# Gated cross-attention and six local-attention layers on one core: a new order of work in a slot, LayerNorm input half in place, logits in pairs

## What is computed

```python
x = x + tanh(g_xattn) * xattn(layernorm(x), ctx, ctx, fside, ...)   # softmax(QK' + bias) V, 16 heads of 8
h = layernorm(x)
for i in range(6):
    h = attn_layer(shift_tokens(h), Wqkv[i], q_scale[i], k_scale[i], Wo[i]) + h
    h = ffn_layer(shift_tokens(h), ln_g[i], ln_b[i], W1[i], b1[i], W2[i], b2[i]) + h
x = x + tanh(g_ffn) * h
# attn_layer: q, k = l2norm(.) * scale, rotary; per window of 32: softmax(8 q k' + mask) v
# ffn_layer: layernorm, W1 -> (a, gate), a * gelu(gate) @ W2;  shift_tokens moves half of the features by one token
```

## Time and profile before

| | |
|---|---|
| median of 3 runs | 2069.49 us (2068.37 to 2073.53) |
| profiled execution, its own time | 2061.48 us |
| its span | 2059.7 us |
| mean granted TensorE clock | 0.972 of 2.4 GHz |
| busy: PE, PEld | 1797.2 us (87%), 1401.8 us (68%) |
| busy: DVE, ACT, POOL | 1600.0 (78%), 1384.6 (67%), 1332.1 us (65%) |
| chain that ended last | PE 60%, DVE 15%, issue 12%, ACT 6%, POOL 5% |

### The profile page before, as it was taken

One profiled execution on the slowest core, in us unless ns is written; L12 is line 12 of the kernel. 1 busy time (PEld: TensorE's weight loads), 2 busy tenths in 40 slices (PEclk: granted clock), 3 DMA queues, 4 the chain that ended last, 5 costly groups with the idle time before them and its releaser, 6 DMA issues.

```text
span 2059.7 us, 86637 instructions
## 1 busy us (share of the span) xinstructions
PE 1797.2 (87%) x33584; PEld 1401.8 (68%) x33584; DVE 1600.0 (78%) x3772; ACT 1384.6 (67%) x3701; POOL 1332.1 (65%) x1226
## 2 busy tenths in 40 slices
PE   6999878998879898789988899988898988899887
PEld 3445457777667776677776677776677776677766
DVE  5766679898468987488896589885689885689984
ACT  3677657777557776567775577775577775577765
POOL 3444467777467777377775477774677773677773
PEclk9999979999989999999999999999899999899999
DMA  5000021111021111111110211110211110211111
GB/s 121 4 5 5 1 70 33 35 37 32 25 64 41 31 36 28 63 34 33 40 31 23 68 40 31 41 31 23 64 44 31 31 42 22 65 37 37 31 33 46
DMA packets 59120, 77.81 MB, mean 38 GB/s; under 512 B 16608, under 2 KB 31674, under 8 KB 57914
## 3 DMA queue, kind: packets, MB, share of 16 engines
q1 hardware_dynamic: 58938, 75.36, 13.9%
HBM read 22.63 MB, written 1.05 MB: 11 GB/s over the span
## 4 chain that ended last, share of the span: by engine, by line
PE 60%; DVE 15%; issue 12%; ACT 6%; POOL 5%; SPq 0%; DMA 0%; DVEq 0%; ACTq 0%; POOLq 0%
PE proj_ps L455 7%; PE s_ps L476 7%; PE tr_ps L465 7%; PE y_ps L524 7%; PE proj_ps L457 5%; PE proj_ps L456 5%; PE y_ps L516 4%; DVE by_cos L1091 3%; PE pv_ps L506 3%; ACT square L816 3%; DVE by_sin L1091 3%; DVE xs L1352 3%; PE s_ps L571 3%; DVE sumsq L1103 2%; PE s_ps L691 2%
## 5 line engine op out<-in xcount | busy, mean ns | idle before, releaser
L1502 POOL TENSOR_TENSOR qk<-by_cos,by_sin 128x512 f32<-128x512 f32 x388 | 495.3, 1276 | 208.3 <-DVE by_sin L1091 201.9
L1509 POOL TENSOR_TENSOR qk<-qk,inv_norm 128x512 f32<-128x512 f32 x388 | 404.8, 1045 | 68.7 <-ACT inv_norm L822 41.6
L1091 DVE TENSOR_TENSOR by_cos<-proj_ps,tab 128x512 f32<-128x512 f32 x364 | 249.4, 685 | 159.6 <-ACT square L816 158.6
L816 ACT ACTIVATE square<-proj_ps 128x512 f32<-128x512 f32 x364 | 217.4, 597 | 195.1 <-PE proj_ps L457 194.8
L1515 POOL TENSOR_TENSOR s_sb<-s_sb,row_max 128x512 f32<-128x512 f32 x192 | 202.7, 1056 | 136.1 <-DVE row_max L1122 136.1
L455 PE MATMUL proj_ps<-w_hi,x_hi 128*128 128x512 f32 x546 | 273.8, 502 | 4.8 <-DVE by_sin L1091 2.6
L465 PE MATMUL tr_ps<-ident,qk 128*128 128x128 f32 x1544 | 247.2, 284 | 24.2 <-ACT x_hi L810 11.8
L1103 DVE TENSOR_REDUCE sumsq<-square 128x8 f32<-128x512 f32 x388 | 262.2, 676 | 0.0
L1091 DVE TENSOR_TENSOR by_sin<-proj_ps,tab 128x512 f32<-128x512 f32 x364 | 247.8, 681 | 0.0
L465 PEld LDWEIGHTS tr_ps<-ident,qk 128*128 128x128 f32 x1544 | 184.0, 146 | 72.5 <-POOL qk L1509 28.5
L457 PE MATMUL proj_ps<-w_hi,x_lo 128*128 128x512 f32 x546 | 222.1, 407 | 0.0
(11 more groups left out here) (172 smaller groups left out, 4167.1 us busy)
## 6 DMA issues: line engine op xcount, KB each, us to landing
arena<-v SPq DMA_DIRECT2D x388, 130.0 KB, 2.4
w_raw<-in_L_ffn_Wqkv SPq DMA_DIRECT2D x7, 1536.0 KB, 7.3
wo<-in_L_ffn_Wo SPq DMA_DIRECT2D x7, 512.0 KB, 3.8
w_raw<-in_L_ffn_W SPq DMA_DIRECT2D x7, 341.0 KB, 5.5
c_in<-in_ctx SPq DMA_DIRECT2D x16, 64.0 KB, 1.8
xn<-in_fside_BxS SPq DMA_DIRECT2D x1, 1024.0 KB, 6.0
out<-z SPq DMA_DIRECT2D x4, 256.0 KB, 3.0
w<-in_L_ffn_W SPq DMA_DIRECT2D x12, 64.0 KB
```

Source lines behind the costliest of these rows:

```text
L1091: return dve.tensor_tensor(dst[:, c % 2, :].rearrange("p (h d) -> p h d", d=DH), ps, tb, ALU.mult)
L1502: pool.tensor_tensor(heads(qk[:, c, :]), heads(by_cos[:, c % 2, :]), heads(by_sin[:, c % 2, :])[:, :, ::-1, :], ALU.add).then_inc(qk_added, 1)
L1509: pool.tensor_tensor(ap, ap, inv_norm[:, c, :].unsqueeze(2).to_broadcast([128, 8, DH]), ALU.mult).then_inc(qk_ready, 1)
```

## The change

Four things. (1) In a layer's slot each of the four engines gets another order of its calls. TensorE does projection 1 ahead of the transpose of chunk 3, projection 2 ahead of the first attention transpose, and projection 5 ahead of the values; VectorE puts the sum of squares between the two rotations for chunks 0 and 3, the second mask ahead of the rotations of chunk 2 with its maxima behind them, `ln_apply` in the middle of the slot; ScalarE and GpSimd follow. (2) LayerNorm: the unshifted half is no longer copied to `xs`; statistics are taken of each half apart and joined, and the application becomes two `scalar_tensor_tensor` of 64 columns, whose second tensor is `rstd` broadcast along the row. (3) In the x stage the scores are made for two groups at once, with the two logits matmuls (32 rows each, next row groups) beside each other: bias g, logits g, logits g + 1, bias g + 1. The second pair's first logits matmul waits for mask g - 1 too. (4) The scores and values matmuls stay on tiles of 64x32.

```diff
             def x_scores(T, par, g):
...
+                x_bias(T, par, g, True)
                 if g == 0:
                     pe.wait_ge(xk_ready, T + 1)
-                rows = slice(32 * g, 32 * g + 32)
-                pe.matmul(s_ps[:, g % 2, :], xq[rows, par, :], flat(xk_bd[rows, par]), start=False, stop=True).then_inc(s_full, 1)
+                if after(T, 1) or g >= 2:
+                    pe.wait_ge(masked, T * 4 + g)
+                x_logits(T, par, g, False).then_inc(s_full, 1)
+                x_logits(T, par, g + 1, True)
+                x_bias(T, par, g + 1, False).then_inc(s_full, 1)
...
                 def ln_stats(T, n, par):
-                    zt = tile_of(z, n, 0, D // 2)
                     dve.wait_ge(sh_full, T + 1)
-                    dve.tensor_scalar(xs[:, par, 0:D // 2], zt, 1.0, None, ALU.mult).then_inc(xs_ready, 1)
-                    dve.tensor_copy(xs[:, par, D // 2:D], y_ps[:, 0:D // 2]).then_inc(xs_ready, 1)
-                    dve.wait_ge(xs_ready, T * 2 + 2)
-                    dve.bn_stats(stats[:, par], xs[:, par]).then_inc(stat_done, 1)
+                    dve.tensor_copy(xs[:, par], y_ps[:, 0:D // 2]).then_inc(xs_ready, 1)
+                    dve.bn_stats(stats[:, par, 0], tile_of(z, n, 0, D // 2))
+                    dve.wait_ge(xs_ready, T + 1)
+                    dve.bn_stats(stats[:, par, 1], xs[:, par]).then_inc(stat_done, 1)
...
                 def ln_apply(T, n, par):
                     dve.wait_ge(rstd_ready, T + 1)
-                    dve.tensor_scalar(tile_of(xn, n), xs[:, par],
-                                      mean_var[:, par, 0:1], rstd[:, par:par + 1], ALU.subtract, ALU.mult).then_inc(xn_ready, 1)
+                    for lo, src in ((0, tile_of(z, n, 0, D // 2)), (D // 2, xs[:, par])):
+                        last = dve.scalar_tensor_tensor(tile_of(xn, n, lo, lo + D // 2), src, mean_var[:, par, 0:1],
+                                                        rstd[:, par:par + 1].to_broadcast([128, D // 2]), ALU.subtract, ALU.mult)
+                    last.then_inc(xn_ready, 1)
```

More of the change, by code:

```diff
@@ L554, in x_project, with x_bias, x_logits @@
                 pe.matmul(proj_ps[0][:, 256:384], xc_T[:, 1], xw_T[:, 2], start=True, stop=True).then_inc(xproj_full, 1)
+            def x_bias(T, par, g, first):
+                hi, lo = flat(pos_hi[:, GH * g:GH * g + GH]), pos_lo[g]
+                pe.matmul(s_ps[:, g % 2, :], d_hi[:, par], hi, start=first, stop=False)
+                pe.matmul(s_ps[:, g % 2, :], d_hi[:, par], lo, start=False, stop=False)
+                return pe.matmul(s_ps[:, g % 2, :], d_lo[:, par], hi, start=False, stop=not first)
+            def x_logits(T, par, g, first):
+                rows = slice(32 * g, 32 * g + 32)
+                return pe.matmul(s_ps[:, g % 2, :], xq[rows, par, :], flat(xk_bd[rows, par]), start=first, stop=not first)
             def x_scores(T, par, g):
@@ L599, in x_slot @@
                     x_values(T - 1, 1 - par, 1)
-                x_scores(T, par, 1)
-                if not first:
                     x_p_transpose(T - 1, 3)
@@ L1395, in slot @@
                         add_out(T - 2, n - 2)
-                    step(T, 0, behind, front_on)
-                    if behind >= 2:
-                        ln_stats(T - 2, n - 2, par)
+                    mask(T, 0)
+                    row_maxima(T, 0)
                     if not front_on:
@@ L1401, in slot @@
                         w_round(0, L + 1)
-                    step(T, 1, behind, front_on, stats_ready=T - 1 if behind >= 2 else None)
+                    if front_on:
+                        times_cos(T + 1, 0, L - 1)
+                        sum_squares(T + 1, 0)
+                        times_sin(T + 1, 0, L - 1)
+                        clamp_norm(T + 1, 0)
+                    if behind >= 2:
+                        ln_stats(T - 2, n - 2, par)
+                    if front_on:
+                        times_cos(T + 1, 1, L - 1)
+                        times_sin(T + 1, 1, L - 1)
+                        sum_squares(T + 1, 1)
@@ L1403, in slot @@
+                    if behind >= 1:
+                        sums_inverse(T - 1, 1)
+                    if behind >= 2:
+                        dve.wait_ge(stat_done, T - 1)
+                    if behind >= 1:
+                        normalise(T - 1, 1)
                     if behind >= 2:
                         ln_variance(T - 2, par)
+                    if front_on:
+                        clamp_norm(T + 1, 1)
+                    mask(T, 1)
+                    if not front_on:
+                        w_round(1, L + 1)
@@ L1409, in slot @@
-                    step(T, 2, behind, front_on)
-                    if not front_on:
-                        w_round(2, L + 1)
-                    step(T, 3, behind, front_on)
+                    if front_on:
+                        clamp_norm(T + 1, 2)
                     if behind >= 2:
                         ln_apply(T - 2, n - 2, par)
+                    if front_on:
+                        times_cos(T + 1, 3, L - 1)
+                        sum_squares(T + 1, 3)
+                        times_sin(T + 1, 3, L - 1)
+                        clamp_norm(T + 1, 3)
@@ L1416, in _ @@
+                    sums_inverse(T, 0)
+                    normalise(T, 0)
                 layer_slots(dve.Fori, L, slot)
```

139 lines of the change are left out of this document (65 added, 74 removed).

## The result

| | before | after |
|---|---|---|
| median, runs of the same chip in turn | 2068.93 us (4 runs) | 1961.05 us (1959.82 to 1963.80, 4 runs) |
| ratio | | 0.9484, 95% interval 0.9453 to 0.9514 |
| span of the profiled execution | 2059.7 us | 1958.7 us |
| mean granted clock | 0.972 | 0.969 |

A forecast was written before the change was run, and what follows sets the result against it. A ring of waits between TensorE and VectorE, neither full, was taken as the bound. Savings of 58 + 24 + 19 = 101 us took the profiled 2061.48 us to 1960; 8 us for the median gave 1968 us, range 1935 to 2020.

The forecast's parts named there:

- The ring: Steady slots: TensorE and VectorE wait for each other through the `xs` copy; 15.35 us falls to 14.6, 58 us less.
- steps 2 and 3: Steady slots: TensorE's 1.3 us stall for `xs` goes; waits for `by_sin` and GpSimd's scaling then set 14.6 us.
- LayerNorm's form: LayerNorm on VectorE: one half read in place, two applications of 64 columns; the 0.76 us copy falls away.
- step 1: VectorE's steady slot: without the 0.76 us copy its own work falls from 13.87 us to about 13.1.
- the first rival: Steady slots: the second LayerNorm application waits for a whole GpSimd scaling; 15.0 us a slot, 2000 us in all; chance 0.21.
- Exclusion: VectorE and GpSimd take turns at SBUF; the two-tensor application does not avoid it and buys nothing over a scalar one.
- step 5: Steady slots on VectorE: `z_stage` waits 0.3 us for GpSimd, the first application 0.9, the second not at all.
- The margin of 0.2 us: Steady slots: the second LayerNorm application asks 0.2 us before GpSimd's next scaling is ready.
- Slots 0, 1, 15: Each layer's first two slots and slot 15: 4 us less a layer, 24 us in sum; none to 36.
- The x stage: Cross-attention stage: paired logits save 1.8 us of TensorE a slot, but 1.3 reaches the period; 19 us less, 8 to 33.
- the period: Cross-attention slot: mask of set 2 at 7.4 us, then the chain to the output projection; 12.2 us against 13.5.
- The sum: Whole kernel: 58 us from steady slots, 24 from slots 0, 1 and 15, 19 from cross-attention, 101 us less.

The follow-up runs named there:

- the squares last: Chunk 0's sum of squares behind `by_sin`: in the changed kernel 0.9602; with `x_att_T` copied early and both LayerNorm applications later as well, 0.9302 of the kernel before.
- the order alone: The changed kernel with the old LayerNorm (both halves copied, one application of 128 columns): 0.9509 of the kernel before.
- the scalar form: The changed kernel with LayerNorm's two applications taking two scalars by pointer and one tensor: 0.9477 of the kernel before.
- the copy moved: The changed kernel with ScalarE copying `x_att_T` right behind p of set 0, ahead of the exponentials of set 2: 0.9372 of the kernel before.
- the pairs alone: The kernel before with only the cross-attention stage's logits put in pairs: 0.9966 of the kernel before.
- the added products: The changed kernel with nine unused identity products on TensorE in every cross-attention slot: 0.9377 of the kernel before.
- LayerNorm alone: The kernel before with only LayerNorm's first half read in place and applied in two pieces, old orders: 1.0113 of the kernel before.

## Why the prediction was right, and where it was not

- **The ring** (steps 2 and 3) held. The wait for `xs` went; projection 2 waits 0.23 us for `by_sin` (0.3 forecast). The transpose of chunk 1 starts 9.83 us after the scores (9.88). The slot came out at 14.4 instead of 14.6, as what follows that transpose takes 4.57 us and not 4.74. VectorE's own work was added up wrong (13.87 − 0.76 and two terms of 0.1 are 13.3, not 13.1), without effect, as VectorE is not the bound. The two runs with the squares last showed that the sum of squares of chunk 0 costs 0.17 us of the slot, which the forecast had in its walk. What the 78 slots gave, 71 us, stands against 58.
- **LayerNorm's form** (step 1) gives nothing. The forecast let its 0.76 us fall away from VectorE, true of the old order; with the order alone the copy costs 0.19 us and the slot is the same. Put into the old order it made the kernel slower, by the same lost turn that was the first rival.
- **Exclusion** (step 5) was right in place and size: `z_stage` 0.43 us (forecast 0.5), first application 1.00 (1.0), second 0.27 (0.15). That the two-tensor form doesn't escape it is shown by the scalar form's 967 ns against 999. The margin of 0.2 us was real, if 0.34 us, and moving one sum of squares used it up.
- **Slots 0, 1, 15** were put at 24 us. The stretches that hold them gave 14.8 + 5.5 + 2.8 = 23 us. Their split among the slots was not tested.
- **The x stage** is the step that failed: 19 us forecast, 6.5 measured. The pair itself was right (1.05 us saved, 0.9 taken). Two parts of the reasoning were not, and a third effect was not in it.

First, the period. The chain from the mask of set 2 to the next output projection was right, 4.36 us for 4.43. But that mask was to start 7.4 us into a slot, which with the projection's own 0.35 is 7.75 us behind the projection's start; in the two slots at full clock shown above it starts 8.75 and 8.40 us behind it. Between the two pairs TensorE now waits at the transposes of set 3 for GpSimd's scaling, whose inverse sums stand behind the mask of set 0 on VectorE; the forecast had no such wait. So the period was 12.93 us and not 12.2. TensorE and VectorE in the slot that starts at 105.42:

```profile
110.51 0.66 PE L485 MATMUL pv_ps<-ident,p_sb 128*128 128x128 f32 x4 [0.60 <-POOL p_sb L1536]
```
```profile
114.17 1.12 DVE L1219 SCALAR_TENSOR_TENSOR s_sb<-d_neg,alpha,s_ps 128x128 f32<-128x128 f32 x4 [0.81 <-PE s_ps L564]
```

With the copy moved the same slots take 11.73 us and 14 intervals 162 us: 21.6 us less than before, about the term's size.

Second, the clock was taken as given. TensorE was busy for 12.8 of 13.5 us of a slot and for 10.6 of 12.9 after; four slots then ran at a granted clock of 0.77 or 0.78 and cost some 2.4 us each, so that 14 slots took 3 us more than before.

Third, the stage still ended sooner, as its first slots now ran at the full level while before they did not. Logits in the kernel before, in the one with the pairs alone (here a pair), and a pair in the changed kernel:

```profile
39.93 2.07 PE L571 MATMUL s_ps<-gelu,xq 32*128 32x512 f32 x2
```
```profile
40.36 2.07 PE L564 MATMUL s_ps<-gelu,xq 32*128 32x512 f32 x4
```
```profile
43.31 1.13 PE L564 MATMUL s_ps<-gelu,xq 32*128 32x512 f32 x4
```

In the nine profiles of kernels that have both the pairs and the new orders the first bias matmul at full speed starts at 30 to 34 us; in the four without pairs, and in the one profile with the pairs alone, at 48 to 51. This start is worth some 9 us, more than the whole stage gained, and no part of the forecast. What brings it forward was not tried.

- **The sum**, 101 us, came out at 101 because 13 us too little in the steady slots met 12.5 too many in the x stage: that is luck. The 8 us between the profile and the median, which the forecast carried over to the changed kernel, were not there again; so it came out at 1961 and not 1968. In the five profiles of the changed x stage with the new orders it ends 5 to 9 us sooner than before, around the low end of the term's 8 to 33; with the added products it is 16 us, with the copy moved 31.

## What to carry to other kernels

When the pacing wait of a ring is found, walk on to the wait that comes next before pricing the edit: in the old order it and a lost turn took back more than the missing copy gave. Where two engines take turns at a resource, price the order of the requests and the margin between them: the same edit cost 23 us with a margin of 0.34 us and gave 11 to 16 us without the clash. And where an edit takes work off TensorE but not off the period, look at the granted clock of each slot, since the idle time can cost what the shorter work gave.

## What the runs showed of the hardware that was not expected

**Idle time on TensorE lowered its clock.** Nine small products a slot, 2 us of work, took every drop away up to the stage's last interval, which is low in every kernel here. In the Trainium skill, TensorE: Matmul & The Clock Gate, "Part 1: The HAM clock gate (the "warmup" mystery)", says that the gate follows how busy the array has been and that the clock is at one of two levels only; by that a stretch at 0.78 is a mean over both (1.2 and 2.4 GHz). The trace agrees: of the slot at 144.40 (0.78) the first pair of logits took 2.08 us, the second 1.13.

```profile
146.26 2.08 PE L564 MATMUL s_ps<-gelu,xq 32*128 32x512 f32 x4
...
154.10 1.13 PE L564 MATMUL s_ps<-gelu,xq 32*128 32x512 f32 x4
```

**A slot can settle into a pattern of two.** With LayerNorm alone 15.18 and 16.05 us in turn, with the squares last 14.23 (often 15.02) and 14.82: a lost turn makes the slot long, and in the next one the request may fall into a gap again. A mean over slots hides this; the starts of one line show it.

**Each layer but the first begins with a stall on TensorE that nothing in the program explains.** Its first 64 score matmuls wait for "issue" (no event that the profile shows), once or twice. First the kernel before, then the changed kernel, then the one with the added products:

```profile
1166.88 1.10 PE L476 MATMUL s_ps<-k_T,q_T 64*32 64x64 f32 x62 [3.25 <-issue]
1169.61 0.42 PE L476 MATMUL s_ps<-k_T,q_T 64*32 64x64 f32 x2 [1.63 <-issue]
```
```profile
823.80 1.13 PE L476 MATMUL s_ps<-k_T,q_T 64*32 64x64 f32 x60 [2.96 <-issue]
826.36 0.43 PE L476 MATMUL s_ps<-k_T,q_T 64*32 64x64 f32 x4 [1.42 <-issue]
```
```profile
1090.36 1.17 PE L476 MATMUL s_ps<-k_T,q_T 64*32 64x64 f32 x64 [2.91 <-issue]
```

The second break falls after 62 matmuls, after 60, or is missing. It is after 62 in all five layers of the four kernels without pairs, two of them with other edits in the layers, and after 60 in all nine profiles with the pairs and without the products; only what TensorE has earlier in its program goes with it. It takes 1.4 to 5.3 us. Where it is missing, five boundaries between layers took 320.3 us, and 333.7 in the changed kernel's run of the same group: about the 13 us that the added products gave outside their stage; the five second breaks of that run are 8.2 us of it. The other profiles with the new orders have 330 to 344 us there. Whether the loading of TensorE's instructions is behind it was not tried. Until it is known, a difference of half a per cent between two kernels with different TensorE instructions may have nothing to do with the edit's own aim, and the steady slots are the better measure of it.
